# Attention and feed-forward in one program on 8 cores: column groups in ten slots, feed-forward from slot 58, bias copied by GpSimd

## What is computed

```python
# step 1: attention in a band of 256 keys, 16 query heads, 2 key/value heads of 64
q, k, v = x @ Wq + bq, x @ Wk + bk, x @ Wv + bv
scores[t, w] = q[t] . k[t - 128 + w]          # w = 0 .. 255, keys outside are zero rows
x = layernorm(x + softmax(scores) @ v_window @ Wo + bo)
# step 2: channel mixing with the row before
xp = x shifted down by one row
xr, xk = mu_r * x + (1 - mu_r) * xp, mu_k * x + (1 - mu_k) * xp
x = layernorm(x + sigmoid(xr @ W_r.T) * (square(relu(xk @ W_k.T)) @ W_v.T))
```

## Time and profile before

| | |
|---|---|
| median of 3 runs | 470.42 us (469.24 to 470.93) |
| the profiled execution itself | 471.38 us |
| its span on the slowest core, core 5 | 469.8 us |
| spans of cores 0 to 7 | 466.4, 463.0, 461.6, 463.6, 467.6, 469.8, 463.2, 466.4 us |
| mean granted TensorE clock of the cores | 0.970 (core 5) to 0.981 (core 2) |
| busy on core 5: VectorE, ScalarE, GpSimd | 309.1, 322.1, 103.5 us |
| DMA | 61.72 MB, 131 GB/s |

### The profile page before, as it was taken

How to read it: one execution, slowest core, us unless ns; L and a number is a source line. 1 busy time by engine, 2 the same in 40 slices (tenths; PEclk the granted TensorE clock), 3 DMA queues, 4 the chain that set the end, 5 groups by cost and what they waited for, 6 DMA issues and landing times.

```text
span 469.8 us, 10062 instructions; the slowest of 8 cores (461.6 to 469.8 us)
## 1 busy us (share of the span) xinstructions
PE 415.2 (88%) x2878; PEld 211.7 (45%) x2878; DVE 309.1 (66%) x781; ACT 322.1 (69%) x835; POOL 103.5 (22%) x240
## 2 busy tenths in 40 slices
PE   0768998799988984999999989998999998999992
PEld 0444443354444442464454453363455454465640
DVE  0045665665665595687898897896797886661913
ACT  1165866958676856587699488769589859547353
POOL 3201202204040111021140142132123123331302
PEclk9997998989999997799999999999999999999998
DMA  7999995397989797648487859565858766613022
GB/s 95 160 168 212 167 162 102 69 197 139 146 147 171 85 119 136 127 80 168 73 144 153 195 83 219 104 143 127 192 100 169 162 108 159 157 24 113 0 91 90
DMA packets 88117, 61.72 MB, mean 131 GB/s; under 512 B 77312, under 2 KB 77440, under 8 KB 88064
## 3 DMA queue, kind: packets, MB, share of 16 engines
q1 hardware_dynamic: 80720, 36.20, 36.1%
q0 software_dynamic: 7344, 24.87, 33.3%
HBM read 49.76 MB, written 8.39 MB: 124 GB/s over the span
## 4 chain that ended last, share of the span: by engine, by line
PE 55%; ACT 12%; DMA 12%; DVE 9%; issue 8%; POOL 2%; SPq 1%; ACTq 0%; DVEq 0%; POOLq 0%
PE pm L343 10%; PE pm L363 9%; PE pm L331 8%; PE pm L373 8%; PE pm L353 5%; PE po L398 5%; PE psc L286 4%; ACT p L437 4%; DVE nmax L590 4%; DMA yT<-qy 3%; DMA zx<-bo 3%; DMA bufq<-wq 2%; DMA bufx<-xt 2%; PE pm L325 2%; PE pm L310 2%
## 5 line engine op out<-in xcount | busy, mean ns | idle before, releaser
L437 ACT ACTIVATE p<-psc,nmax 128x320 bf16<-128x320 f32 x264 | 138.7, 541 | 85.3 <-DVE nmax L590 84.4
L590 DVE TENSOR_REDUCE nmax<-psc 128x2 f32<-128x640 f32 x132 | 108.1, 821 | 75.9 <-PE psc L292 75.6
L331 PE MATMUL pm<-bufx,bufq 128*128 128x512 bf16 (+2 forms) x320 | 68.0, 360 | 3.0 <-DMA bufq<-wq 2.8
L343 PE MATMUL pm<-w16o,ao 128*128 128x512 bf16 x272 | 65.5, 384 | 3.0 <-ACT vt L483 1.4
L602 DVE TENSOR_SCALAR p<-p,rall 128x320 bf16<-128x320 bf16 x264 | 62.5, 300 | 7.2
L353 PE MATMUL pm<-bufx,w16kf 128*128 128x256 bf16 x512 | 60.5, 273 | 0.2 <-DVE bufx L674 0.2
L363 PE MATMUL pm<-w16r,bufx 128*128 128x512 bf16 x256 | 59.7, 380 | 0.0
L373 PE MATMUL pm<-w16vf,bufq 128*128 128x512 bf16 x256 | 59.3, 380 | 0.0
L437 ACT ACTIVATION_READ_ACCUMULATOR p<-psc,nmax 128x1 f32 x264 | 57.5, 218 | 0.0
L353 PEld LDWEIGHTS pm<-bufx,w16kf 128*128 128x128 bf16 x512 | 48.4, 98 | 11.0 <-issue 4.1
L286 PE MATMUL psc<-k,qy 64*128 64x320 bf16 x264 | 41.5, 311 | 12.6 <-ACT p L437 9.4
(11 more groups left out here) (80 smaller groups left out, 527.4 us busy)
## 6 DMA issues: line engine op xcount, KB each, us to landing
zx<-bo SPq DMA_DIRECT2D x17, 512.0 KB, 4.9
zx<-xres POOLq DMA_DIRECT2D x17, 512.0 KB, 6.2
out<-zb SPq DMA_DIRECT2D x15, 512.0 KB, 3.3
bufx<-xt POOLq DMA_DIRECT2D x6, 512.0 KB, 9.9
bufq<-wq POOLq DMA_DIRECT2D x4, 512.0 KB, 10.1
w16o<-wo POOLq DMA_DIRECT2D x4, 512.0 KB, 13.3
w16kf<-wkf POOLq DMA_DIRECT2D x4, 512.0 KB, 11.0
w16r<-wr POOLq DMA_DIRECT2D x4, 512.0 KB, 8.1
```

What stands on the lines that cost most here:

```text
L331: mm = e.matmul(pm[:, bank, 0:QHI[a] - QLO[a]], wq[b // 2][:, kc, 128 * (b % 2):128 * (b % 2) + 128], xt[a][:, kc, QLO[a]:QHI[a]], start=( ...
L343: mm = e.matmul(pm[:, bank, :], ao[:, a % 2, kc, :], w16o[:, kc, 512 * b:512 * b + 512], start=(kc == 0), stop=(kc == KC - 1))
L437: a = e.activation(p16[:, b % 2, j // 2, g, j % 2, :], psc[:, 2 * (n % 2) + g, 0:320], AF.Exp, bias=nmax[:, n % 4, g:g + 1], accum_out=sal ...
L590: e.tensor_reduce(nmax[:, n % 4, :], psc[:, 2 * (n % 2):2 * (n % 2) + 2, 0:320], mybir.AxisListType.X, ALU.max, negate=True).then_inc(s_mx, 1)
```

## The change

- Each column group takes ten slots in place of twelve: K, V, q0, then both W's and q1 in one slot, then q2 to q7. The starts become 4, 20, 34 and 46, and the second half of it all moves up: `F0` is 58, so there are 168 slots.
- The halves of x4 are loaded in slots 33 and 36 in place of 36 and 37.
- The k mixes of the last pair are put four to a slot, in place of two.
- VectorE normalises P after the second sums and the mixes of a slot, in place of before them.
- The bias is loaded once into `bo32`. GpSimd copies it into `zx` (`fill`) two slots after y of the tile two before, and starts the residual DMA three slots after it.
- The two halves of a pair's transposed y count on semaphores of their own, and a half waits only for the half before it in the same place.
- The scratch tile `junk` is gone: the squares of zx are written to the place of `qy` where y of the tile comes afterwards, those of zb to `th[r % 2]` (float32); the tanh that next writes there waits for them.

```diff
@@ -20,7 +20,7 @@
 NH = 8
-F0 = 60
+F0 = 58
 FP = 13
@@ -28,7 +28,7 @@
 QHI = (384, 512, 512, 512, 320)
-GSLOT = (None, 4, 22, 36, 48)
+GSLOT = (None, 4, 20, 34, 46)
 BT = 11
@@ -47,9 +47,10 @@
         free = [n for n in range(GSLOT[g], NSLOT) if n not in (15, 16, 18, 19)]
-        us = [("K", g, 0), ("V", g, 0), ("W", g, 0), ("W", g, 1)] + [("q", g, dc) for dc in range(8)]
+        us = [[("K", g, 0)], [("V", g, 0)], [("q", g, 0)], [("W", g, 0), ("W", g, 1), ("q", g, 1)]]
+        us += [[("q", g, dc)] for dc in range(2, 8)]
         for n, u in zip(free, us):
-            todo.setdefault(n, []).append(u)
+            todo.setdefault(n, []).extend(u)
     ffn = [("k", j) for j in range(4)] + [(a, t, nh) for a in "rv" for t in range(2) for nh in range(2)]
@@ -114,7 +115,7 @@
     slots = dict(zip(at, order))
-    slots.update({36: ("x", 4, 0), 37: ("x", 4, 1)})
+    slots.update({33: ("x", 4, 0), 36: ("x", 4, 1)})
     return slots
@@ -133,7 +134,7 @@
         for c in range(8):
-            slots.setdefault(n + 1 + c // 2, []).append(("k", h, c))
+            slots.setdefault(n + 1 + (c // 2 if h < NH - 1 else c // 4), []).append(("k", h, c))
             slots.setdefault(n + (5 + c // 2 if c < 4 else 3 + c), []).append(("r", h, c))
@@ -206,7 +207,7 @@
     zb = sb("zb", [128, 2, D], F32)
-    junk = sb("junk", [128, D])
+    bo32 = sb("bo32", [128, D], F32)
     mask = sb("mask_s", [128, 2, 64])
@@ -243,7 +244,7 @@
     d_cols, d_mask, d_ident = sem("d_cols"), sem("d_mask"), sem("d_ident")
-    d_bo = [sem("d_bo%d" % j) for j in range(2)]
+    d_bo = sem("d_bo")
     d_wk, d_wv, d_wo = sem("d_wk"), sem("d_wv"), sem("d_wo")
@@ -251,7 +252,7 @@
     d_pt = [[sem("d_pt%d%d" % (r, j)) for j in range(2)] for r in range(2)]
-    d_yT = [sem("d_yT%d" % j) for j in range(2)]
+    d_yT = [[sem("d_yT%d%d" % (j, i)) for i in range(2)] for j in range(2)]
@@ -262,7 +263,7 @@
-    s_p, s_ln1, s_ln2 = sem("s_p"), sem("s_ln1"), sem("s_ln2")
+    s_p, s_ln1, s_ln2, s_fl = sem("s_p"), sem("s_ln1"), sem("s_ln2"), sem("s_fl")
@@ -484,6 +485,7 @@
                     e.wait_ge(s_ed, DVE_COUNT[INDEX[("v", a - 2, 1)]])
+                    e.wait_ge(s_sq2, a - 1)
                 e.activation(th[a % 2][:, 512 * b:512 * b + 512], src, AF.Tanh,
@@ -515,7 +517,8 @@
                 e.wait_ge(s_ln1, tau - 1)
-            e.activation(junk[:, :], zx[:, tau % 2, :], AF.Square,
+            e.activation(qy[:, tau, :, :].rearrange("p a b -> p (a b)"), zx[:, tau % 2, :], AF.Square,
                          accum_out=st1[:, tau % 2, 2:3]).then_inc(s_sq1, 1)
@@ -532,6 +535,8 @@
                 e.wait_ge(s_ln2, r - 1)
+            junk = th[r % 2]
             if r < 2 * NH - 1:
@@ -655,9 +660,10 @@
             par = h % 2
-            e.wait_ge(d_yT[par], 16 * (2 * (h // 2) + 2 + par))
+            for half in range(2):
+                e.wait_ge(d_yT[par][half], 16 * (h // 2 + 1 + par * half))
             if h == 0:
-                e.wait_ge(d_yT[1], 16)
+                e.wait_ge(d_yT[1][1], 16)
             if h < 2:
@@ -683,9 +689,6 @@
                 max_step(n + 1)
-            b, i = divmod(n - 1, 4)
-            if 0 <= b < NB and i in (0, 2):
-                normalise(b, i // 2)
             h, i = divmod(n - F0 - 12, FP)
@@ -702,6 +705,9 @@
                     mix_r(h, c)
+            b, i = divmod(n - 1, 4)
+            if 0 <= b < NB and i in (0, 2):
+                normalise(b, i // 2)
             for u in SLOT[n]:
@@ -716,8 +722,13 @@
+        def fill(tau):
+            if tau >= 2:
+                e.wait_ge(s_y, tau - 1)
+            e.tensor_copy(zx[:, tau % 2, :], bo32[:, :]).then_inc(s_fl, 1)
         def add_xres(tau):
-            e.wait_ge(d_bo[tau % 2], 16 * (tau // 2 + 1))
+            e.wait_ge(s_fl, tau + 1)
             e.dma_start(zx[:, tau % 2, :], xres.ap()[128 * tau:128 * tau + 128, :],
@@ -756,6 +767,9 @@
         wo_piece(3)
+        e.wait_ge(d_bo, 16)
+        for j in range(2):
+            fill(j)
         for j in range(2):
@@ -798,8 +812,10 @@
                 scale(st1[:, tau % 2, :], False, tau == 0, s_ln1)
-            if n - 4 in YOUT[:NT - 2]:
-                add_xres(YOUT.index(n - 4) + 2)
+            if n - 2 in YOUT[:NT - 2]:
+                fill(YOUT.index(n - 2) + 2)
+            if n - 3 in YOUT[:NT - 2]:
+                add_xres(YOUT.index(n - 3) + 2)
             if n in LOADS:
@@ -824,8 +840,7 @@
         e.wait_ge(d_xt[1], 32)
-        for j in range(2):
-            e.dma_start(zx[:, j, :], bo_in.ap()).then_inc(d_bo[j], 16)
+        e.dma_start(bo32[:, :], bo_in.ap()).then_inc(d_bo, 16)
@@ -837,12 +852,12 @@
-        def y_transpose(tau, par, col, before):
+        def y_transpose(tau, par, half, before):
             e.wait_ge(s_y, tau + 1)
             if before >= 1:
-                e.wait_ge(d_yT[par], 16 * before)
-            e.dma_start(yT[:, par, :, 16 + col:144 + col], qy[:, tau, :, :],
-                        transpose=True).then_inc(d_yT[par], 16)
+                e.wait_ge(d_yT[par][half], 16 * before)
+            e.dma_start(yT[:, par, :, 16 + 128 * half:144 + 128 * half], qy[:, tau, :, :],
+                        transpose=True).then_inc(d_yT[par][half], 16)
@@ -850,17 +865,13 @@
                 if tau == 0:
-                    y_transpose(0, 1, 128, 0)
+                    y_transpose(0, 1, 1, 0)
                     continue
                     e.wait_ge(s_pc, h)
-                y_transpose(tau, par, 128 * half, 2 * (h // 2) + par + half)
-            if n - 1 in YOUT[:NT - 2]:
-                tau = YOUT.index(n - 1)
-                e.wait_ge(s_y, tau + 1)
-                e.dma_start(zx[:, tau % 2, :], bo_in.ap()).then_inc(d_bo[tau % 2], 16)
+                y_transpose(tau, par, half, h // 2 + par * half)
             if n - 1 in FIN:
```

## The result

Over four runs each, the changed kernel took 481.43 us in the median (477.96 to 482.83) and the kernel before 469.83 (465.88 to 470.93): a ratio of 1.0251, 95% interval 1.017 to 1.0333: slower beyond doubt, by about 2.5%. The forecast was 463.6 with a range of 456.5 to 470.5, so both the size and the direction are wrong. The profiled execution took 482.83 us. Each time in this document is the median of all executions of a kernel, and each ratio is taken only over those in which no cores fell into a slower state at a lower granted clock.

A forecast was written before the change was run, and what follows sets the result against it. TensorE's standing and half-clock time, mostly gaps in the first third, was taken to bound the kernel. On core 5, −20.5 + 11.6 + 3 − 3 + 1.2 = −7.7 gave 462.1, about 462 plus 1.6: 463.6 us, range 456.5 to 470.5.

The forecast's parts named there:

- the first groups: First third: q1.7 earlier −1.99, slots 20 and 21 filled −1.2, W waits −1.49, −1.77, −1.36; clock −1.7 twice.
- the queue stalls: GpSimd's bias wait gone, −1.33 on core 5; SyncE's hold before block 12 gone, −5.68 and −3.3 of clock, less 1.
- rival (b): Block 12: stall stays because the DMA engines, not SyncE's order, set it; +8, 471 us, no change; chance 0.08.
- the 9 us for block 12: Late transposed P of block 12 on core 5: stall removed, −5.68 and −3.3 of clock.
- the squeezed groups: Light slots: 30 to 33 +3.2, 44 and 45 +2.0, 52 to 57 +1.8; merged W slots +4.2 over all groups.
- rival (c): Light slots worse, gaps and clock: 3 us in slots 30 to 33, 2 at 44 and 56; +5, 468.5 us; chance 0.10.
- The fill: GpSimd's 17 bias copies, 1.25 us each, sometimes holding VectorE: +3, bounds 0 and 19.
- The end: Last projection to y 16: less work between, but a shorter chain: +1.2, bounds 0 and 3.5.
- The fastest cores: Cores at 461.6 us shed the first groups' 11.2, pay 11.6 and 1.2, and stay near 462.
- normalising later, −3: VectorE, 230 to 410 us: second sums come earlier, so ScalarE waits less for them; −3, bounds 0 and −6.
- the feed-forward runs two slots ahead: Second half: feed-forward moved up two slots, while y 16 still hangs on the last projection at slot 139; +1.2 at the end.
- the list of signs: Expected in the profile: no bias wait, block 12 gap under 1.5 us, W gaps at most 1, cores within 4 us.

The follow-up runs named there:

- e10: The kernel before with only the own semaphores for the halves of y: 469.69 us, ratio 1.0005 to the kernel before.
- e9: The change with the old schedule and P normalised early, bias copy and own semaphores kept: 464.15 us, ratio 0.9847 to the kernel before.
- e7: The change with the same group starts, but V transposes and q1 in slots of their own: 473.53 us, ratio 1.0024 to the kernel before.
- e12: The change with groups spread, final rows early, P normalised early, residual DMA two slots later, then every bias copy made three times: 466.47 us, 0.9909 to kernel before.
- e4: The change with P normalised before the second sums and mixes again: 476.53 us, ratio 1.0108 to the kernel before.
- e2: The change with the old schedule put back, late normalising, bias copy and own semaphores kept: 467.36 us, ratio 0.9948 to the kernel before.
- e3: The change with the final rows always placed as early as allowed (reach of one slot, not three): 473.29 us, ratio 1.0064 to the kernel before.
- e1: The kernel before with only the new schedule (ten-slot groups, F0 58, x4 loads, last k mixes): 474.87 us, ratio 1.0124 to the kernel before.

## Why the prediction was wrong, point by point

By its own steps, core 5 before against core 1 after (the slowest of each), time lost by PE:

| stretch | forecast | measured |
|---|---|---|
| slots up to 13 | +0.8 | 15.0 to 13.7: −1.3 |
| slots 14 to 29 | −6.9 | 8.1 to 1.6: −6.5 |
| slots 30 to 59 | −2.8 | 14.1 to 16.2: +2.1 |
| from slot 60 | +1.2 | 11.2 to 28.4: +17.2 |
| sum | −7.7 | +11.5 (span +11.4) |

The core 5 of before is the slowest in one execution and core 1 after in another, so the last row of the two is partly the choice of cores; the measured times differ by 11.6 us as well.

- **Right: the first groups.** q1.7, slots 20 and 21 and the W's of group 2 with their clock: −6.5 for −6.9.
- **Right: the queue stalls.** No bias wait, no wait of SyncE on a y transpose, no stall at block 12; rival (b) fell. But the semaphores have no part in the time (e10), and the 9 us for block 12 were those of one core in one execution: no core in e10's table row has it (3.3 us at most in slots 46 to 59), and the time is the same, since other cores stand just behind.
- **Mis-sized: the squeezed groups.** With copy and semaphores on the old schedule (e9), slots 30 to 59 lose 5.3 us, of which 3.1 are the W waits that the schedule removes; the change loses 16.1 there. So the new schedule costs some 14, where my terms for these slots sum to 9.6 (3.2 + 2.0 + 1.8 + 2.6): 4.4 too little, which is about the 5 that rival (c) asked for. Spreading the groups (e7) takes 9.3 of the 14 back. The place isn't that of rival (c), though. Slots 57 and 58 with the half clock behind them (187 to 192 us) lose 6.0 us on core 1, against 1.8 in the forecast, and are most of the miss: I carried slack behind slots 50 and 51 into them, but PE had none to give: it had waited 3.2 us itself in slots 49 and 50 (core 1).
- **Mis-sized: the fill.** Copy 1.03 us for the 1.25 taken; cost some 2 us by e12, for the 3 taken. Right within its bounds.
- **Right: the end.** +1.2 forecast, 1.5 measured (1.1 to 2.6 us in slots from 132 on).
- **A slip in the sum.** The fastest cores were said to stay near 462 us; 461.6 − 11.2 + 11.6 + 1.2 is 463.2. It changes the forecast by little over 1 us.
- **Failed, sign: normalising later, −3.** It costs about 1% (e4 to the change; e9 to e2). I counted only who reads the second sum sooner and forgot who is behind the normalisation: a P transpose on SyncE, and behind that the y transpose, which on some cores then loses its place against the residual DMA; and that in the new order the normalisation itself stands behind the wait for y.
- **Failed, the step that decided: "the feed-forward runs two slots ahead", at no cost from slot 60 on but at the end.** I moved the work but not the planner's answer: the final rows of block 0 came out 4 slots closer to the evacuation that overwrites their place, those of block 1 3 slots. The cover that I should have named was the 5 or 6 slots that an output DMA had. And I credited the bias DMA's absence to the stall alone, where it also lets the residual DMA start beside the y transpose. Together this is 8 us on core 1 in slots 72 to 84 (7.5 in slot 83, where output projection 9 had moved to and which I had booked among the credits) and, with the late normalising, 7 in slots 124 to 131. The runs show that it takes both parts of the change: in slots 72 to 84 the schedule alone loses 3.1 us, the rest alone 1.0, the change 6.9, and with the final rows early 0.9.

The cores ended 11 us apart, where the list of signs had 4, and that was the plainest sign that one wait differed from core to core. The two signs that I had named for a wrong forecast, fills over 2 us and the gap of block 12, didn't come: the cause lay where I had none.

What stayed open: why the issue of one P transpose is sometimes longer; how the cost of late normalising divides between the queue of SyncE and VectorE's own order; how much of e3's gain is the final rows and how much y 8's slot; and the 1.5 us at the end (1.9 us at the first k unit of the last pair, slot 149, in every kernel with `F0` 58), whose cause was not tried by itself.

## What to carry to other kernels

When an edit feeds a planner, run the planner by hand on both versions and compare the distance of every pair (last reader, next writer), above all where a DMA is the reader: here 6 slots became 2 and nobody had touched them. Taking a wait away from a queue also takes away the spacing it gave; ask which transfers now start together, and fix their order by the event that each waits for, not by slot numbers. For eight cores judge by the core that is worst after the edit: a stall of one core in one profile is worth no more than its distance to the next core.

## What the hardware showed that I had not expected

**Which of two DMAs leaves first goes with what both take.** The y transpose before took 3.3 us in the median, with the residual DMA some 7 us away from it. The same transpose of y 8 over all eight cores of a kernel:

| | residual DMA leaves | y 8 took | output 1 took |
|---|---|---|---|
| change | 0.15 to 0.31 us ahead | 6.7 to 12.2 us | 6.7 to 11.8 us |
| e4 | 0.17 behind | 5.2 to 6.3 | 6.4 to 7.2 |
| e3 | 0.8 to 1.5 behind | 3.1 to 3.3 | 3.1 to 3.4 |
| e1 | 6.8 to 7.3 behind | 3.3 to 4.1 | 5.5 to 5.9 |

The kernels differ in more than that, but y 14 shows the same within one kernel: in the change it took 3.3 to 3.7 us on the seven cores on which it left 0.4 to 0.65 us ahead, and 6.8 on the one on which it left 0.33 behind. The distance counts too: on ten cores of e2 and e9 y 14 left 0.3 to 0.5 us ahead and took about 5 to 6 us. The DMA engines moved only 139 GB/s in the window of y 8 on core 1, against 157 before, so it isn't the bytes. The Trainium skill, "DMA: Bandwidth & Descriptors", section "Queues, rings and completion order", says that a DMA engine takes turns between the queues it has work for, a packet each. That residual DMA, transpose and output stretch together (10.3, 10.6 and 9.96 us at y 8 on core 1) agrees with it; that the first to leave should matter so much doesn't follow from it, and no run here shows why.

**GpSimd's copy does hold VectorE, by whole instructions, and only some of them.** One line each of the change on core 1 (duration min/median/max in ns): the copy, the normalising of P and the second sum:

```profile
L728 POOL COPY zx<-bo x17: 1028/1034/1162, 45.0 to 400.0; 128x1024 f32<-128x1024 f32 x17
```

```profile
L607 DVE TENSOR_SCALAR p<-p,rall x264: 283/299/1072, 29.2 to 415.5; 128x320 bf16<-128x320 bf16 x132
```

```profile
L645 DVE SCALAR_TENSOR_TENSOR zb<-zb,qy x15: 1207/1219/1877, 227.3 to 469.5; 128x1024 f32<-128x1024 f32 x15
```

Before, the longest normalisation was 0.373 us; beside a copy it is up to 1.07. On core 1 of the change six of VectorE's instructions beside a copy are stretched, by 3.5 us in all: two normalisations, one second sum and three mixes, all of them reading SBUF alone. The maxima and the evacuations of v, which read PSUM, keep their length although 14 of them fall beside a copy. This agrees with the exclusive port lock of "SBUF — State Buffer", section "Who interferes with whom", in the Trainium skill, which the forecast weighed. In the kernel's time a copy costs 0.11 to 0.13 us (e12), an eighth or less of its length, since few copies meet an instruction that they hold and VectorE has time to spare.
